# Inverse square roots of the norms computed as a power on GpSimd, with the order of all engines planned anew

## The reference

```
x = x + attnA(layernorm(x), ctx)      # two products with kv, rows normalised, softmax
x = x + ffn0(layernorm(x))            # dense gelu FFN 512-2048-512, plus the best 2 of 8 experts
                                      # of width 256, each part rms-normed, their sum rms-normed
x = x + attnB(layernorm(x), ctx, ctx) # rms-norm of q and k, rotation, 16 heads over 4 kv groups, causal
x = x + ffn1(layernorm(x))            # dense silu FFN 512-2048-512
```

## Time and profile before

| | |
|---|---|
| median of 3 runs | 1782.6 us |
| profiled execution | 1781.71 us |
| its span | 1780.0 us |
| mean granted TensorE clock | 0.965 |
| PE busy | 1655.6 us, 93% |
| DVE busy | 1130.1 us, 63% |
| ACT busy | 820.1 us, 46% |
| POOL busy | 270.1 us, 15% |

### The profile page before, as it was taken

The page is one execution under the profiler, slowest core; times in us unless marked ns, Lnnn a source line. Parts: engine busy times, 40 slices in busy tenths (PEclk is TensorE's granted clock), DMA queues, the critical chain, the costliest instruction groups (busy, mean ns, idle before and its releaser), DMA issues. The chain is left out here.

```text
span 1780.0 us, 27304 instructions
## 1 busy us (share of the span) xinstructions
PE 1655.6 (93%) x9204; PEld 1328.9 (75%) x9204; DVE 1130.1 (63%) x2748; ACT 820.1 (46%) x1803; POOL 270.1 (15%) x301
## 2 busy tenths in 40 slices
PE   3699999799999997999999999998999989999998
PEld 2587788688999985776767766876777667688887
DVE  5788877855776738965777754499565554543222
ACT  3566564244776732325666655332354463421110
POOL 1213221551222113210010100142100000000000
PEclk9599999899999998999999999999999979999999
DMA  3325569498899897879789863788963524345661
GB/s 108 118 95 166 200 229 341 170 339 321 299 359 347 269 344 243 286 262 360 270 280 342 294 238 98 284 303 313 296 216 90 160 72 178 101 161 178 209 217 59
DMA packets 135594, 410.05 MB, mean 230 GB/s; under 512 B 16032, under 2 KB 30752, under 8 KB 131744
## 3 DMA queue, kind: packets, MB, share of 16 engines
q1 hardware_dynamic: 123552, 368.98, 60.1%
q0 software_dynamic: 11904, 39.33, 6.6%
HBM read 303.92 MB, written 104.33 MB: 229 GB/s over the span
## 5 line engine op out<-in xcount | busy, mean ns | idle before, releaser
L1318 PE MATMUL ps<-xT,gu 128*128 128x512 f32 (+1 forms) x1224 | 453.3, 370 | 12.7 <-DVE gu L1834 5.6
L1320 PE MATMUL ps<-xT,gu 128*128 128x512 f32 (+1 forms) x1224 | 441.8, 361 | 0.0
L1319 PE MATMUL ps<-xT,gu 128*128 128x512 f32 (+1 forms) x1224 | 440.8, 360 | 0.0
L1318 PEld LDWEIGHTS ps<-xT,gu 128*128 128x128 f32 x1224 | 233.3, 191 | 49.6 <-issue 11.0
L1318 PE MATMUL ps<-wd,hid 128*128 128x512 f32 x604 | 247.9, 410 | 24.1 <-issue 11.4
L1320 PEld LDWEIGHTS ps<-xT,gu 128*128 128x128 f32 x1224 | 233.0, 190 | 35.3
L1319 PEld LDWEIGHTS ps<-xT,gu 128*128 128x128 f32 x1224 | 233.7, 191 | 29.4
L1319 PE MATMUL ps<-wd,hid 128*128 128x512 f32 x604 | 240.2, 398 | 0.0
L1320 PE MATMUL ps<-wd,hid 128*128 128x512 f32 x604 | 240.2, 398 | 0.0
L1531 ACT ACTIVATE hid<-act 128x512 fp32r<-128x512 f32 (+1 forms) x174 | 99.6, 573 | 246.4 <-DVE act L1819 245.8
L1819 DVE TENSOR_TENSOR act<-act,ps 128x512 f32<-128x512 f32 (+1 forms) x174 | 106.7, 613 | 148.3 <-PE ps L1320 147.8
(11 more groups left out here) (292 smaller groups left out, 2582.4 us busy)
## 6 DMA issues: line engine op xcount, KB each, us to landing
gu<-w_dram SPq DMA_DIRECT2D x150, 512.0 KB, 5.4
raw<-in_ffn_w SPq DMA_DIRECT2D x65, 768.0 KB, 6.0
wd<-w_dram SPq DMA_DIRECT2D x96, 512.0 KB, 5.2
w_dram<-raw SPq DMA_DIRECT2D x48, 512.0 KB, 4.8
gu_third<-w_dram SPq DMA_DIRECT2D x42, 512.0 KB, 3.8
w_dram<-gu SPq DMA_DIRECT2D x16, 1024.0 KB, 8.5
raw<-in_ffn_w POOLq DMA_DIRECT2D x48, 256.0 KB, 5.4
QT<-q_dram SPq DMA_DIRECT2D x48, 256.0 KB, 6.1
```

The source lines that it names most:

```text
L1318: mm(out_ap, ah, bh, start=start, stop=False)
L1319: mm(out_ap, ah, bl, start=False, stop=False)
L1320: return mm(out_ap, al, bh, start=False, stop=stop)
```

## The change

It has two parts. The first moves each root to POOL: DVE writes variance plus epsilon (and, where there is a mean, minus the mean, in a new tensor_scalar) and signals `root_asked`; POOL waits for it, raises to the power of -0.5 in one tensor_tensor, multiplies with minus the mean where there is one, and signals `rooted`; ACT or DVE wait for `rooted`. The scaling by BETA, the three pieces and eight tensors go. The waits on `rows_ready`, `sim_ready`, `rows2_ready`, `k_scaled`, `q_scaled` and `rows4_ready` become waits on `rooted`, and `parts` and `final` on DVE now wait for POOL, where they waited for DVE itself. The second part gives the planner other durations for roots, turns (transposes), scores, exponentials, values and norms, so that all orders change: on PE turn, xgt and kturn go from 0.36 to 0.43 us, rowt, qt and rowt4 from 0.36 to 0.42, values from 0.47 to 0.4, norm from 0.22 to 0.1. In `scores` only the first of two matmuls into one bank now has its start flag; both have the same sizes as before.

```
-    ROOT = 3
+    ROOT = 1
+    ROOT_US = 1.3
-    SHARED |= {("POOL", kind) for kind in ("gam", ..., "qtab")}
+    SHARED |= {("POOL", kind) for kind in ("gam", ..., "qtab", "stats1", "simstats", "stats2", "stats4", "mnorm", "fnorm", "qnorm", "krs")}
-            return [("PE", 0.36), ("ACT", 0.48)] + ([] if a[0] else [("DVE", 0.6)])
+            return [("PE", 0.42), ("ACT", 0.48)] + ([] if a[0] else [("DVE", 0.6)])
-                return {..., "min": [("DVE", (0.18 + 0.134 * wide) * two)], "exp": [("ACT", (0.25 + 0.115 * wide) * two)]}[kind]
+                return {..., "min": [("DVE", (0.08 + 0.134 * wide) * two)], "exp": [("ACT", (0.27 + 0.115 * wide) * two)]}[kind]
-            return [("DVE", (1.2 if kind == "stats1" else 0.6) if a[1] < n else 1.2 if a[1] == n else 0.6 if a[1] < n + ROOT - 1 else 1.0)]
+            return [("DVE", 1.2 if kind == "stats1" else 0.6)] if a[1] < n else [("DVE", 0.85), ("POOL", ROOT_US)]
-            return [("DVE", (1.0, 0.7, 1.1 if kind == "qnorm" else 0.85)[a[-1]])]
+            return [("DVE", 0.55 if kind == "qnorm" else 0.2), ("POOL", ROOT_US)]
...
+            def inverse_root(item, to, of):
+                pool.wait_ge(root_asked, ROOT_ASKED[item])
+                return tt(out=to, in0=of, in1=neg_half[:, 0:of.shape[-1]] if len(of.shape) == 2 else ..., op=ALU.pow)
+            def row_scales(item, rs_, nm_, c=slice(0, TB)):
+                link(inverse_root(item, rs_[:, c], var_of[item[0]][:, c]))
+                tt(out=nm_[:, c], in0=neg_mean[item[0]][:, c], in1=rs_[:, c], op=ALU.mult).then_inc(rooted, 1)
+            link(nc.gpsimd.memset(neg_half[:, :], -0.5))
...
+                elif kind == "mnorm":
+                    inverse_root((kind, *a), rr[:, :, c], v2[:, :, c]).then_inc(rooted, 1)
...
-                        last = mm(ps[:, 4 + p % 2, at:at + cols], ..., start=True, stop=True)
+                        last = mm(ps[:, 4 + p % 2, at:at + cols], ..., start=at == 0, stop=True, skip_group_check=True)
...
+                V_.tensor_scalar(var_of[kind][:, c], mv[kind][:, c, 1], mul, add, ALU.mult, ALU.add)
+                V_.tensor_scalar(neg_mean[kind][:, c], mv[kind][:, c, 0], -1.0, None, ALU.mult).then_inc(root_asked, 1)
...
                 elif kind == "parts":
-                        settled()
+                        dve.wait_ge(rooted, ROOTED["mnorm", b, i // 2, 0])
...
                 elif kind == "final":
-                    settled()
+                    dve.wait_ge(rooted, ROOTED["fnorm", b, i // 2, 0])
```

More of the change, by code:

```diff
@@ L258, in two_layers @@
     SHARED = {("DVE", kind) for kind in ("ctx", "kv", "bet", "resid", "xt", "low", "w", "wo", "esplit", "comb", "parts", "final", "qrow", "split", "weights", "top2", "places", "before")}
-    SHARED |= {("POOL", kind) for kind in ("gam", "xh", "xt", "parts", "qsum", "kprep", "kscale", "qtab")}
+    SHARED |= {("POOL", kind) for kind in ("gam", "xh", "xt", "parts", "qsum", "kprep", "kscale", "qtab", "stats1", "simstats", "stats2", "stats4", "mnorm", "fnorm", "qnorm", "krs")}
     MOVED = {"eload": (0, 256, 1), "estore": (1, 512, 0), "raw": (1, 768, 0), "pre": (1, 512, 0), "wstore": (2, 1536, 0), "xs": (0, 512, 4), "xtload": (1, 2048, 0), "xload": (1, 1024, 0), "x1store": (1, 1024, 0),
@@ L925, in two_layers, with asks_root @@
         ROWS = [i[1:] for i in SCHED if i[0] == "rown"]
+        def asks_root(item):
+            return item[0] in ("mnorm", "fnorm", "qnorm", "krs") or item[0] in ("simstats", "stats2", "stats4") and item[2] == TB or item[0] == "stats1" and item[2] == 2
+        ROOT_ASKED = {i: n + 1 for n, i in enumerate(i for i in ORDERS["DVE"] if asks_root(i))}
+        ROOTED = {i: n + 1 for n, i in enumerate(i for i in ORDERS["POOL"] if asks_root(i))}
         MIN_NO = {i[1:]: n + 1 for n, i in enumerate(i for i in SCHED if i[0] == "min" and not masked_on_dve(i[2]))}
@@ L1273, in _ @@
                 elif kind == "kscale":
-                    pool.wait_ge(k_scaled, 1)
+                    pool.wait_ge(rooted, ROOTED["krs", 0])
                     for b in range(B):
@@ L1758, in link, with row_scales @@
                     settled()
[L1760 to L1775, removed]
+            def row_scales(kind, mul, add, first=0, n=TB):
                 settled()
                 c = slice(first, first + n)
[L1779 to L1786, removed]
-                    settled()
-                    stt(out=nm_[:, c], in0=mv[kind][:, c, 0], scalar=-1.0, in1=rs_[:, c], op0=ALU.mult, op1=ALU.mult).then_inc(done, 1)
+                for i in range(first, first + n):
+                    last = V_.bn_aggr(mv[kind][:, i, :], st[kind][:, i, :])
+                link(last)
+                V_.tensor_scalar(var_of[kind][:, c], mv[kind][:, c, 1], mul, add, ALU.mult, ALU.add)
+                V_.tensor_scalar(neg_mean[kind][:, c], mv[kind][:, c, 0], -1.0, None, ALU.mult).then_inc(root_asked, 1)
             def over_e(a_):
```

112 lines of the change are left out of this document (55 added, 57 removed).

## The result

The changed kernel takes 1741.43 us (median of 4 runs, 1736.31 to 1749.34) against 1782.26 us before: 41 us less, a ratio of 0.976 (95% interval 0.9738 to 0.9782). I had forecast 1764.6 us, with a range from 1744 us. The direction was right, and the gain was more than twice what I had summed up. The profiled execution is the fastest of the four, 1736.31 us with a span of 1734.1 us.

A forecast was written before the change was run, and what follows sets the result against it. It took PE, busy 1655.6 of 1780.0 us, as the bound, with DVE nearly full in the mid stretches. Mid stretches 15.0, clock 1.5 and start 1.5 gave 18.0 us off, so 1764.6 us; range 1744 to 1790 us.

The forecast's parts named there:

- DVE is relieved of 32.6 and 30.3 us in the mid stretches: Both stretches of mid work: root instructions and their pauses leave DVE, whose busy share of the first falls from 88% to 63%.
- Mid stretches: half of PE's idle time, 15.0 us: Both stretches of mid work: half of PE's 29.9 us idle time there is won, 9.4 + 5.6 = 15.0 us.
- The rival in which nearly all is won: Mid stretches, clock and start: DVE no longer delays any tile, 33 us won, 1750 us; chance 0.15.
- Clock: 1.5 us: Both mid stretches: 1.5 us won from PE time lost to a lower granted clock, as between 672 and 680 us.
- Start: 1.5 us: First image: three roots on the path, each 0.4 us shorter, and a little DVE work: 1.5 us won.
- All other roots at nothing: Later images' stats1 to stats4 and krs: no cost, since they go beside PE work not waiting for them.
- A root costs POOL 1.3 us: POOL: power and multiplication take 1.3 us a root, between bounds of 0.64 and 2.6 us; 41 roots add 53 us.
- The new orders: 0, with 8 us either way: All queues: changed planner durations nearly cancel, 0 us, from 8 us won to 8 us lost.
- The port gives half back: Mid stretches: POOL's added two-input work blocks DVE, halving the relief; 9 us won, 1774 us; chance 0.18.
- POOL's queue, slower: mnorm and fnorm roots stand behind gathers on POOL, so DVE waits 5.6 us each time; 1796 us; chance 0.16.
- The gaps of 6.15 and 5.47 us gone or under 2 us: Sign of being right: PE's gaps before 675.2 and 709.7 us, in mid work, vanish or fall under 2 us.
- Wrong altogether if the attention stretch or the start changed by over 8 us: Sign of being wrong: over 8 us change in the attention stretch or the start, counted at 0 and 1.5 us.

The follow-up runs named there:

- the load put back: Changed kernel and its order, with nine chained small scratch instructions on DVE behind each of the 41 root requests: 1775.32 us, ratio 0.9947.
- kernel planned heavy: Changed kernel's instructions, with the planner told that each root still takes 2.5 to 2.9 us of DVE: 1784.57 us, ratio 1.0003.
- the two kernels with less PE work: Kernel before and changed kernel, each with 128 matmuls left out in 8 second-layer dense tiles of image 1: 1783.01 and 1740.08 us.
- the load at the other roots: Changed kernel, with the scratch DVE instructions only behind the 17 requests of stats1, simstats, stats2, stats4 and krs: 1749.59 us, ratio 0.9812.

## Why the prediction was right or wrong

- *DVE is relieved of 32.6 and 30.3 us in the mid stretches.* Right in kind, and the load put back there confirms that it counts. DVE's busy time fell by 21 and 26 us (104.14 to 83.17, 108.64 to 82.38), in stretches that also hold fewer matmuls (463 to 443, 504 to 433). The mid stretches became shorter by 21.6 and 20.3 us, two thirds of the relief in each; of that the load put back takes 13 and 11 us, and some 9 us each stay with the order.
- *Mid stretches: half of PE's idle time, 15.0 us.* This is the step that failed. I valued the relief by the idle time of PE inside the stretch, as if PE's work were the bound everywhere and the mid work delayed nothing behind it. Taken by itself the 15.0 us were near: PE's idle time in the two stretches fell by 18.6 us (18.8 to 4.5, 11.3 to 7.0). But the chain of side work was the bound, and what it gained came through whole: PE also saved 9.4 us of idle time and by my estimate 9.5 us of clock between 1400 and 1450 us, where I did not look. The kernel planned heavy has little PE idle time left in its mid stretches and gains nothing; the two kernels with less PE work are no faster. The term should have been the shortening of the stretch, 42 us. The rival in which nearly all is won, at 1750 us, came nearest, but by the same wrong measure.
- *Clock: 1.5 us.* Looked for in the wrong place. PE's same matmuls took 19.7 us less, but by busy time times missing clock the two mid stretches lost 6.6 us before and still 6.0 us after. Between 672 and 680 us, where I had expected 1.00, the clock is 0.71:

```profile
672.00:680.00 8.00, 8.00 (x27) 6.36 (x26) 5.10 (x9) 0.72 (x2) 7.01 (x8) 0.71 0.35 96
```

  About half of the 19.7 us is the place from 1400 to 1450 us, again an effect of the late chain; the rest is spread.
- *Start: 1.5 us.* Somewhat small. The path from the scaled variance to ACT is now 31.53 to 33.01 us, 1.5 us where I had said 1.6:

```profile
31.36 0.17 DVE L1801 TENSOR_SCALAR s_varsimstats<-mv_simstats 128x4 f32<-128x4 f32 x1
...
31.68 1.01 POOL L1205 TENSOR_TENSOR s_rsim<-s_varsimstats,neg_half 128x4 f32<-128x4 f32 x1 [18.56 <-DVE s_neg_meansimstats L1802]
...
32.77 0.20 POOL L1210 TENSOR_TENSOR s_nmsim<-s_neg_meansimstats,s_rsim 128x4 f32<-128x4 f32 x1
33.01 2.78 ACT L1662 ACTIVATE va<-ps,s_nmsim,s_rsim 128x512 f32<-128x512 f32 x4 [6.65 <-POOL s_nmsim L1210]
```

  The first dense tiles come some 4 us earlier than before (73.2 us against 77.7), but by 110 us nothing of it is left, and the first mid stretch begins only 1 us earlier. *All other roots at nothing*: too low, but by little. Of the 8 us that the load at the other roots costs, some 5 us arise by 130 us, most of them in the first 100, and 2 to 3 us in the 50 us behind that.
- *A root costs POOL 1.3 us.* Near: 1.0 + 0.2 us for 4 columns. POOL's busy time rose by 48.4 us, where I had added 53.
- *The new orders: 0, with 8 us either way.* Right for the durations of turns and attention (ratio 0.9998), wrong for the durations of the roots: without the order that belongs to it, the relief gives nothing, 43 us from the changed kernel. I had treated the plan as noise about the instructions' cost, when it decides whether time saved on an engine is passed on.
- *The port gives half back.* It did not. The DVE groups that both kernels have were busy for 11 us more in all, the most among them in the mid stretches being the sum of expert rows (columns as in the earlier trace rows), before and after:

```profile
L2049 DVE SCALAR_TENSOR_TENSOR ya<-yb,wgt,ya 128x512 f32<-128x512 f32 x16 | 12.0, 751 | 0.6
```

```profile
L2056 DVE SCALAR_TENSOR_TENSOR ya<-yb,wgt,ya 128x512 f32<-128x512 f32 x16 | 15.4, 963 | 0.6
```

  Of DVE's instructions of at most 16 columns 22 took over 1 us before and two do now, and both ran beside a wide product or sum of POOL. Beside a power there was none. More than that, 20 DVE instructions with two SBUF inputs began while a power ran and took their usual time. The clearest case is the longest power, lines picked from the timelines of POOL and DVE:

```profile
284.08 2.90 POOL L1205 TENSOR_TENSOR krs<-k_v,neg_half 128x16 f32<-128x16 f32 x1 [5.54 <-DVE k_v L2046]
...
284.49 0.29 DVE L2009 TENSOR_TENSOR r_key<-lg,r_oh 128x128 f32<-128x128 f32 x1
...
285.02 1.28 DVE L1848 TENSOR_TENSOR gu<-raw,gu 128x512 fp32r<-128x512 f32 x2
286.22 0.69 DVE L1848 TENSOR_TENSOR wd<-raw,wd 128x512 fp32r<-128x512 f32 x1
```

  A subtraction of this size takes 0.68 us in the median of 130. The Trainium skill's rule on the shared pair (SBUF, State Buffer; SBUF's two separate sides) is that a VectorE instruction with two SBUF inputs and a GpSimd instruction that reads SBUF shut each other out for a whole instruction. For wide sums this case agrees (2.23 us in the earlier trace rows), but for a power of a few columns it does not: there DVE went on at its usual pace, and the measurement decides.

- *POOL's queue, slower.* It did not come about. In the changed kernel's list of waits, DVE waited for a root of POOL twice, for 0.4 us in all:

```profile
DVE dn L2067 <- POOL p_r L1205: 0.4, 2, 0.2
```

- *The gaps of 6.15 and 5.47 us gone or under 2 us.* The second is gone, but I had tied it too firmly to a root. Between the root that ended at 705.64 us and the held-up step at 706.74 us, DVE did two instructions on expert rows (705.56 to 706.82 us), and the subtraction itself waited 0.76 us for ACT. The first has become 3.52 us, not under 2 us, at a place with the same releaser:

```profile
671.32 0.79 PE L1355 MATMUL ps<-wd,hid 128*128 128x512 f32 x1 [3.52 <-DVE acc L1868]
```

- *Wrong altogether if the attention stretch or the start changed by over 8 us.* They did not: 355 to 352 us between the mid stretches, 651 to 650 us ahead of them.

## What to carry to other kernels

Where fixed queues interleave a main stream with a side chain, as here, idle time of the busiest engine need not say what bounds a stretch or what a relief is worth: measure the length of the side chain's stretches, and look for the later place where the main stream runs out of work. Leave out some of the main stream's work ahead of that place; if the time does not move, the side chain is the bound. And when an operation gets cheaper under a planned order, the plan has to be told: here the saving was lost whole without it.

## What the hardware showed that I had not expected

A power by tensor_tensor on POOL goes by the column (durations min/median/max in ns):

```profile
L1205 POOL TENSOR_TENSOR rf<-s_varfnorm,neg_half x8: 692/735/1154, 676.4 to 1195.3; 128x2 f32<-128x2 f32 x8
L1205 POOL TENSOR_TENSOR s_rs<-s_varstats,neg_half x12: 1003/1006/1381, 11.8 to 1527.1; 128x4 f32<-128x4 f32 x12
L1205 POOL TENSOR_TENSOR krs<-k_v,neg_half x1: 2898/2898/2898, 284.1 to 284.1; 128x16 f32<-128x16 f32 x1
```

From the least times, 0.69 us for 2, 1.00 us for 4 and 2.90 us for 16 columns, that is about 0.16 us a column and 0.38 us beside it. It suits a few numbers for each row; a tile of 512 columns would by these numbers, as an estimate, take some 80 us. While a power ran, DVE's instructions with two SBUF inputs kept their usual time, as shown above. The multiplication behind it took 0.20 us, less than the 0.32 us that I had set as the lower bound from a tile of 64 columns.
